# A chain of attention and deformable convolutions: the offset convolutions read an image without padding columns, 512 columns a matmul

## The reference

```python
# layer 2: h = relu(bn1(conv1x1(x, w1))), 64 channels; 27 outputs: 18 offsets and 9 masks
off = conv2d(h, woff, stride 1, padding 1) + boff                # woff: (27, 64, 3, 3)
# layer 3, twice: h = relu(group_norm(x)), 256 channels; 18 offsets
f   = depthwise_conv2d(h, dw, 7x7, 'SAME')
off = conv2d(f, pw, 1x1) + pwb                                   # pw: (18, 256, 1, 1)
# both: every pixel takes 9 bilinear samples of h at its own offsets, then a matrix
y, x = base_y + off[:, :, 0], base_x + off[:, :, 1]
samp = bilinear(h, y, x)                                         # four corners, zero outside the image
out  = einsum('bckhw,ock->bohw', samp, w)
```

## Time and profile before

| | |
|---|---|
| time, median of 3 runs | 6705.33 us (6679.31 to 6709.67) |
| profiled execution: span, first to last instruction | 5987.5 us |
| profiled execution's own time | not given apart from its span; the median is 717.8 us above the span |
| PE busy | 5187.2 us (87%) |
| DVE busy | 4250.2 us (71%) |
| POOL busy | 3228.6 us (54%) |
| ACT busy | 2265.2 us (38%) |
| offset matmuls of layer 3 (L738) | 1792 records, 433.3 us busy |
| offset matmuls of layer 2 (L738) | 192 records, 56.6 us busy |

### The profile page before, as it was taken

One profiled execution on the slowest core, in us unless ns is written; L12 is line 12 of the kernel. 1 busy time (PEld: TensorE's weight loads), 2 busy tenths in 40 slices (PEclk: granted clock), 3 DMA queues, 4 the chain that ended last, 5 costly groups with the idle time before them and its releaser, 6 DMA issues. The chain is left out here.

```text
span 5987.5 us, 83281 instructions
## 1 busy us (share of the span) xinstructions
PE 5187.2 (87%) x24252; PEld 2620.8 (44%) x24252; DVE 4250.2 (71%) x7123; ACT 2265.2 (38%) x4090; POOL 3228.6 (54%) x2826
## 2 busy tenths in 40 slices
PE   7999999997676788878879999999977767888788
PEld 3333333333665544644433333333336655446444
DVE  5888888873223599579858888888732235995798
ACT  2444444441112156235524444444411122662355
POOL 0666666661773277147606666666617732771476
PEclk9999999997787899989989999999977878999899
DMA  1000000001333599579900000000013335995799
GB/s 54 1 1 1 1 1 1 1 1 35 105 105 106 189 410 410 177 272 410 371 32 1 1 1 1 1 1 1 1 37 105 105 110 193 410 410 172 277 410 364
DMA packets 310971, 790.59 MB, mean 132 GB/s; under 512 B 69512, under 2 KB 136401, under 8 KB 310222
## 3 DMA queue, kind: packets, MB, share of 16 engines
q0 software_dynamic: 193536, 679.59, 29.7%
q1 hardware_dynamic: 117198, 107.99, 6.2%
HBM read 701.57 MB, written 85.87 MB: 132 GB/s over the span
## 5 line engine op out<-in xcount | busy, mean ns | idle before, releaser
L615 POOL TENSOR_TENSOR arena<-arena 128x512 f32<-128x512 f32 x960 | 1407.5, 1466 | 828.9 <-ACT arena L1115 764.7
L697 POOL DMA_INDIRECT arena<-corners,arena x1152 | 1086.7, 943 | 993.3 <-POOLq L696 706.7
L1115 ACT ACTIVATE arena<-ps 128x1024 f32<-128x1024 f32 x1024 | 1049.5, 1025 | 1239.2 <-PE ps L840 1209.7
L1564 DVE TENSOR_REDUCE arena<-ps 128x2 f32<-128x1024 f32 x1024 | 1243.3, 1214 | 347.1 <-PE ps L814 347.1
L1046 PE MATMUL ps<-arena 128*128 128x512 f32 x2304 | 1065.3, 606 | 3.3 <-PEq L1043 3.2
L840 PE MATMUL ps<-arena 64*128 64x512 f32 x4096 | 1046.0, 589 | 0.0
L1748 DVE SCALAR_TENSOR_TENSOR ps<-arena,ps 128x256 f32<-128x256 f32 x2304 | 956.9, 483 | 108.1 <-DVEq L1742 69.8
L853 PE MATMUL ps<-arena 128*64 128x512 f32 x4096 | 991.3, 605 | 0.0
L1586 DVE TENSOR_TENSOR arena<-arena 128x512 f32<-128x512 f32 x960 | 890.4, 928 | 62.5 <-ACT arena L1115 62.1
L1269 ACT ACTIVATE ps<-arena 128x256 f32<-128x256 f32 x1152 | 503.1, 469 | 625.4 <-DMA arena<-corners,arena 557.6
L652 POOL DMA_INDIRECT arena<-corners,arena x576 | 546.2, 948 | 338.9 <-issue 173.8
(11 more groups left out here) (132 smaller groups left out, 3708.7 us busy)
## 6 DMA issues: line engine op xcount, KB each, us to landing
corners<-arena SPq DMA_DIRECT2D x256, 256.0 KB, 3.9
arena<-corners,arena POOLq DMA_INDIRECT x1728, 2.8
arena<-in_wd SPq DMA_DIRECT2D x4, 2304.0 KB, 8.3
X<-in_x SPq DMA_DIRECT2D x8, 1024.0 KB, 8.4
corners<-arena SPq DMA_DIRECT2D x128, 64.0 KB, 2.2
out_y<-arena SPq DMA_DIRECT2D x32, 256.0 KB, 5.5
arena<-in_base SPq DMA_DIRECT2D x4, 288.0 KB, 9.2
arena<-in_base SPq DMA_DIRECT2D x2, 432.0 KB, 3.1
```

The lines of the kernel that those rows point to most:

```text
L615: pool.tensor_tensor(SUMS[u % 2][:, 0, :], SUMS[u % 2][:, 0, :], P[n % 4][:, 0, :], ALU.add).then_inc(sum_a, 1)
L697: pool.indirect_dma_start(G3[4 * k + t].rearrange("p a c -> p (a c)"), None, table256, bass.IndirectOffsetOnAxis(ap=IS3[:, k, t:t + 1], ax ...
L1115: af(P[n % 4].rearrange("p h q -> p (h q)"), ps[:, 2 * (n % 2):2 * (n % 2) + 2, :].rearrange("p h q -> p (h q)"), ACT.Exp, scale=float(D) ...
L1564: v.tensor_reduce(mxp[i % 2][:, :, j], ps[:, 4:6, :], AX.X, ALU.max).then_inc(mx_done, 1)
```

## The change

The padding columns go. The image is stored with 64 columns and padded above and below only (`HP2` 66 rows, `HP7` 70 rows), so 8 image rows are 512 contiguous columns whatever `ky` is: `rows` is one matmul of 512 columns per `ky` and half, in one PSUM bank. The missing side columns are handled in the shift: DVE starts with the middle `kx`, which covers all 64 columns, and adds the others only where they stay inside the row (61, 62 or 63 columns in layer 3, 63 in layer 2). ACT writes each chunk once, into the image, and PE's table transposes read the image; the staging tiles and the semaphores `image_ready`, `stage_free` and `h1_free` go. POOL clears only the rows above and below. The loops over chunks on PE and ACT are written out.

```diff
-        HP2 = bot.f32(PW2 * PW2, parts=CB)
-        STG2 = [bot.f32(CHUNK, parts=CB) for _ in range(2)]
+        HP2 = bot.f32(ROWS2 * W, parts=CB)
...
-                    pool.memset(HP7.rearrange("p a n -> p (a n)"), 0.0).then_inc(pool_step, 1)
+                    for at in (0, (H + 3) * W):
+                        pool.memset(HP7[:, :, at:at + 3 * W], 0.0).then_inc(pool_step, 1)
...
-                    pe.wait_ge(image_ready, 1)
-                    pe.sem_inc(image_ready, -1)
-                    for j in range(2):
-                        first = True
-                        for half in range(halves):
-                            for ky in range(ksize):
-                                last = mm(ps[0:ko, 2 + 2 * p + j, 0:n], wts(half, ky),
-                                          img(half)[:, bass.ds((8 * blk + 4 * j + ky) * pw_, n)],
-                                          start=first, stop=(half == halves - 1 and ky == ksize - 1))
-                                first = False
-                        last.then_inc(t_ps, 1)
+                    first = True
+                    for half in range(halves):
+                        for ky in range(ksize):
+                            last = mm(ps[0:ko, 2 + p, :], wts(half, ky), img(half)[:, bass.ds((8 * blk + ky) * W, CHUNK)],
+                                      start=first, stop=(half == halves - 1 and ky == ksize - 1))
+                            first = False
+                    last.then_inc(t_ps, 1)
...
-                with act.Fori(0, NCH // 2 - 1) as n2:
-                    for p in range(2):
-                        norm(2 * n2 + 2 + p, p)
...
-                        for half in range(CH):
-                            padded = HP7[:, half, :].rearrange("p (y x) -> p y x", y=PW7)
-                            af(padded[:, bass.ds(8 * n + 3, 8), 3:3 + W],
-                                   src[:, half, chunk(n)].rearrange("p (y x) -> p y x", x=W), ACT.Relu,
-                                   scale=gsc[:, half:half + 1], bias=gbi[:, half:half + 1]).then_inc(act_step, 1)
...
+                    for n in range(NCH):
                         for half in range(CH):
+                            af(HP7[:, half, (8 * n + 3) * W:(8 * n + 11) * W], src[:, half, chunk(n)], ACT.Relu,
+                               scale=gsc[:, half:half + 1], bias=gbi[:, half:half + 1]).then_inc(stage_ready, 1)
...
-                    for kx in range(ksize):
-                        for j in range(2):
...
-                                dve.wait_ge(chain, 2 * (kx - 1) + j + 1)
...
+                    dve.wait_ge(t_ps, 1)
+                    dve.sem_inc(t_ps, -1)
+                    moved = ps[0:ksize * no, 2 + p, :].rearrange("q (y x) -> q y x", x=W)
+                    rows = tbuf[p].rearrange("q (y x) -> q y x", x=W)
+                    mid = ksize // 2
+                    v.tensor_scalar(rows, moved, sel[:, mid:mid + 1], None, ALU.mult).then_inc(chain, 1)
+                    others = [kx for kx in range(ksize) if kx != mid]
+                    for i, kx in enumerate(others):
+                        dve.wait_ge(chain, i + 1)
+                        to = slice(max(0, mid - kx), W - max(0, kx - mid))
+                        at = slice(max(0, kx - mid), W - max(0, mid - kx))
+                        v.scalar_tensor_tensor(rows[:, :, to], moved[:, :, at], sel[:, kx:kx + 1], rows[:, :, to],
+                                               op0=ALU.mult, op1=ALU.add).then_inc(
+                                                   chain if kx < ksize - 1 else t_ready, 1)
```

More of the change, by code:

```diff
@@ L30 @@
 KK = 9
[L31 removed]
+ROWS2, ROWS7 = H + 2, H + 6
 O2, O3 = 27, 18
@@ L156, in program @@
         hole = dcn.at
-        HP7 = dcn.f32(CH, PW7 * PW7)
+        HP7 = dcn.f32(CH, ROWS7 * W)
         after = dcn.at
@@ L171, in program @@
         stg = Carver(dcn.at)
-        STG3 = [stg.f32(CH, CHUNK) for _ in range(2)]
         TS3 = [stg.f32(4, C) for _ in range(2)]
@@ L625, in _ @@
                 pool.sem_inc(go_pool, -1)
-                pool.memset(HP2, 0.0).then_inc(pool_step, 1)
-                pool.wait_ge(pool_step, 1)
-                pool.sem_inc(pool_step, -1)
+                for at in (0, (H + 1) * W):
+                    pool.memset(HP2[:, at:at + W], 0.0).then_inc(pool_step, 1)
+                pool.wait_ge(pool_step, 2)
+                pool.sem_inc(pool_step, -2)
                 pool.memset(IDX2[:, NT:NT + 5, :], 0).then_inc(pool_step, 1)
@@ L757, in offset_conv @@
                 rows(0, 0)
-                def two(n2):
-                    for p in range(2):
[L760 to L773, removed]
+                for n in range(2, NCH):
+                    table(n, n % 2)
+                    rows(n - 1, (n - 1) % 2)
+                    shifted(n % 2)
                 rows(NCH - 1, 1)
@@ L937, in table2 @@
                     for t in range(4):
-                        last = tr(ps[:, 1, t * CB:(t + 1) * CB], STG2[p][:, t * 128:(t + 1) * 128],
+                        last = tr(ps[:, 1, t * CB:(t + 1) * CB], HP2[:, bass.ds((8 * n + 1) * W + t * 128, 128)],
                                   ident_s[0:CB, 0:CB])
@@ L944, in _ @@
                 conv1(0)
-                offset_conv(table2, lambda half: HP2, 1, PW2, 3, lambda half, ky: woff_s[:, ky, :], T2, O2, sel2_s,
-                            written_out=True)
+                offset_conv(table2, lambda half: HP2, 1, 3, lambda half, ky: woff_s[:, ky, :], T2, O2, sel2_s)
                 pe.drain().then_inc(arrived, 1)
@@ L1161, in _ @@
                 act.sem_inc(go_act, -1)
-                def norm2(n, p):
+                for n in range(NCH):
                     act.wait_ge(h1_ready, 1)
                     act.sem_inc(h1_ready, -1)
[L1166 to L1180, removed]
+                    half = slice(n % 2 * CB, (n % 2 + 1) * CB)
+                    af(HP2[:, (8 * n + 1) * W:(8 * n + 9) * W], ps[half, 0, :], ACT.Relu, scale=bnf1[half, 0:1],
+                       bias=bnf1[half, 1:2]).then_inc(stage_ready, 1)
                 act.drain().then_inc(arrived, 1)
@@ L1227, in _ @@
                     act.sem_inc(go_act, -1)
-                    def norm3(n, p):
-                        act.wait_ge(stage_free, 1)
-                        act.sem_inc(stage_free, -1)
+                    for n in range(NCH):
                         for half in range(CH):
-                            af(STG3[p][:, half, :], src[:, half, chunk(n)], ACT.Relu,
-                                   scale=gsc[:, half:half + 1], bias=gbi[:, half:half + 1]).then_inc(stage_ready, 1)
-                        for half in range(CH):
-                            padded = HP7[:, half, :].rearrange("p (y x) -> p y x", y=PW7)
-                            af(padded[:, bass.ds(8 * n + 3, 8), 3:3 + W],
-                                   src[:, half, chunk(n)].rearrange("p (y x) -> p y x", x=W), ACT.Relu,
-                                   scale=gsc[:, half:half + 1], bias=gbi[:, half:half + 1]).then_inc(act_step, 1)
[L1240 to L1246, removed]
+                            af(HP7[:, half, (8 * n + 3) * W:(8 * n + 11) * W], src[:, half, chunk(n)], ACT.Relu,
+                               scale=gsc[:, half:half + 1], bias=gbi[:, half:half + 1]).then_inc(stage_ready, 1)
                     act.drain().then_inc(arrived, 1)
@@ L1433, in group_norm, with table_and_offsets @@
                 dve.sem_inc(dve_step, -1)
-            def table_and_offsets(stage, pv, off, base, ksize, pw_, tbuf, sel, no):
+            def table_and_offsets(stage, pv, off, base, ksize, tbuf, sel, no):
                 def tiles(p):
```

47 lines of the change are left out of this document (10 added, 37 removed).

## The result

The change takes 6653.53 us (median of 8 runs, 6634.97 to 6662.17) against 6685.63 us (8 runs, 6677.64 to 6709.67): a ratio of 0.9943, 95% interval 0.9928 to 0.9958, 32.1 us less. The forecast was 36.4 us less: 6669 us, in a range of 6642 to 6700, from a median of three runs before of 6705.33. Over eight runs that median is 19.7 us lower; counted from there the forecast is 6649.2 us, and the time lies 4.3 us above it.

What follows compares the result with a forecast made beforehand. PE was taken to bound the layer-3 offset stages and SP's table DMAs the layer-2 ones. Terms of -37.4 (PE), +1.6 (DVE) and -0.6 (layer 2) gave -36.4 us: from 6705.3 to 6669 us, range 6642 to 6700.

Steps and rivals of the forecast that it cites:

- Fewer columns, layer 3: PE's layer-3 `rows`, 28 records of 512 columns for 56 of 280: 1.17 us less a chunk, -37.4 us in all.
- Rival D: Layer-3 `rows`: a 512-column record costs 472 ns, so PE gains nothing and the time is 6706 us; chance 0.05.
- the transfers: Layer-3 table tiles: 8.2 us to move and 6.9 to issue, both under a step of 13.8 us, so 0.
- The shift on DVE: Last `block` of each layer-3 stage, now seven chained instructions: +0.4 us a stage, +1.6 us in all.
- the price of a chained wait: DVE's layer-3 `block`: each chained instruction waits 0.15 us, a figure taken from the chain in `corners`.
- Rival C: DVE's `block`: chained waits are free, so the tails give 3.6 us in place of costing 1.6: 6664 us; chance 0.10.
- ACT and POOL: ACT's dropped second pass and POOL's shorter clears were hidden already, so they gain 0.
- the pace: Layer-2 stage: SP's 64 DMAs, 54.76 us without a break, set its length; -0.3 us a stage, -0.6 us in all.
- rival A: Layer-2 stage: less PE work lowers the clock; at 0.50 throughout 22.7 us more a stage, 6714 us; chance 0.08.
- the prediction's own sign: Layer-2 stage expected at 67 to 68 us; more than 3 us off would show the forecast wrong.
- that waits stay while work goes: Layer-2 stage: the change removes PE work and leaves the waits, so the low clock level may come earlier.
- Around the span: Outside the profiled span of 5987.5 us: 717.8 us to the median, not in the trace, taken as unchanged.

Runs made afterwards that it cites:

- Experiment 2: Kernel before with only the four layer-3 offset stages in the new form, layer 2 as before: 5952.15 us, ratio 0.9925 to the kernel before.
- experiment 8: The change with every layer-3 `rows` done twice into the same bank: 6346.74 us, 391.2 more than the change on the same chip.
- experiment 7: The change with ACT's second activations (into unread tiles) and POOL's full clears put back: 5959.32 us, ratio 0.9935 to the kernel before.
- experiment 9: The change with layer-2 `rows` weights zero-padded to 128 rows and 128 columns, image on 128 partitions: 6618.76 us, ratio 0.9903 to the kernel before.
- 10: The change with layer-2 `rows` weights padded to 128 x 128 and table writes split between SP and ACT: 6620.33 us, ratio 0.9909 to the kernel before.
- experiment 6: The change with layer-2 table writes issued half from SP, half from ACT: 5958.41 us, ratio 0.9936 to the kernel before.
- after: Profile of the change itself against the kernel before: this execution took 6634.97 us, median of 8 runs 6653.53 us, ratio 0.9943.
- experiment 3: Kernel before with only the two layer-2 offset stages in the new form, layer 3 as before: 5993.91 us, ratio 0.9993 to the kernel before.
- experiment 4: The change with DVE adding each shift in two halves of four rows, 14 instructions each waiting two back: 5958.11 us, ratio 0.9938 to the kernel before.
- experiment 5: The change again, unedited, on a chip of the short kind: 5955.55 us, ratio 0.9933 to the kernel before.
- 12: The change with layer-2 `rows` weights zero-padded to 128 columns only, 64 rows kept: 6642.40 us, ratio 0.9931 to the kernel before.

## Why the prediction was right, and where not

- **Fewer columns, layer 3: right.** Term -1.17 us a chunk; measured 13.21 - 12.01 = 1.20, -38.4 in all. Experiment 2 has the whole gain there, and experiment 8 shows that nothing else holds the step. Rival D is gone, and so is any doubt about the transfers, which the prediction put at 0: in the steady steps PE never waits for a tile.
- **The shift on DVE: wrong sign, small.** The term +0.4 us for the last block measured -0.2 (5.57 to 5.37). The step that failed is the price of a chained wait, taken from `corners` as 0.15 us where it is 0.04. Rival C had the direction and not the size. Both terms together are -39.2, and the stages fell by 39.5.
- **ACT and POOL: right**, 0 (experiment 7).
- **Layer 2: the pace was right in part, the clock failed.** The prediction let SP's 64 DMAs set the pace and took the clock as unchanged. SP's DMAs are the floor: with the clock up they take 55 of 65 us (experiment 9), and only then does a second queue help (10). At 0.57 halving them on SP changed nothing (6): there PE's work at the granted clock sets the stage. In the profiles the old form takes 69.95, 71.03, 69.95, 71.33, 72.77 and 70.59 us, mean 70.9; the change's form (after, 3, 4, 5, 7, 8) 67.94 to 78.22 us, mean 74.9 of 12. That is +3.9 a stage, +7.9 in all, in place of -0.6.
- **Layer 2: rival A, smaller.** Of the 3.9 us, 1.5 are longer issue on SP (seven of the twelve have 56.4 to 58.9 us, the old form 54.0 to 54.8) and 2.5 come behind its last DMA (10.5 us on average, against 8.0). This is rival A at a clock of 0.54 to 0.73 (the old form has 0.64 to 0.72) and not at 0.50 throughout, so it takes back a fifth of the gain and does not outweigh it. By the prediction's own sign, a layer-2 stage off by more than 3 us, this part was wrong. The size stays open: the old form was profiled on chips of the short kind alone, where the change's ten stages average 75.7 us; the runs of experiment 3 do not confirm a loss (-9.6 to +1.2 us by their interval), while experiment 2, with layer 2 left old, lies 6.0 us below experiment 4 on the same chip, in ranges that overlap. Why the new form sits lower stays open too: that waits stay while work goes was the prediction's argument, and no run tests it by itself.
- **The sum.** -39.5 + 7.9 = -31.6 us by the stages, measured -32.1 and -35.5. Against the forecast of -36.4, PE gave 1.0 us more and DVE 2.4, and layer 2 took 8.5: three misses, two of them against the third. That stages and medians agree to a few microseconds is partly luck, since the eight runs of the change alone span 27 us.
- **Around the span: wrong.** "I take it as unchanged" did no harm, but 1.8 us lie there, not 717.8. The forecast of a difference survived because the 700 us belong to stages that the change doesn't touch, and so carry over just the same. A change to the sampling stages, costed from that profile, would have been sized for the wrong kind of chip.

## What to carry to other kernels

When a profiled span and the medians differ by more than a few microseconds, find out which stages differ before building on either: the two may come from different chips. A stage in which PE is busy at a clock of 0.5 to 0.7 may be bound by that clock, even where a queue issues beside it with hardly a break; the test is to take the queue's work away and see what PE does, and to do it again once the clock is up, for here the queue was the next limit. Where its matmuls use half the rows and columns, padding the weights with zeros to the full array streams no more columns and can be worth more than removing work: here it took a stage to 65.3 us, from 70.9 on a chip of the same kind and 74.9 over all profiles.

## What the runs showed of the hardware

- The same program takes 5991 and 5998 us on two chips and 6686 and 6690 us on two others, the difference all in the sampling stages (414 and 585 us in layer 2). On the long kind PE stands still between its matmuls there for 40.0 of 300 us with nothing in the profile to wait for.
- Busy is not enough for the upper clock: 38 us without a gap at 0.50 (experiment 6). With the records of `rows` on 128 x 128 weights the stage's clock is 0.79 to 0.84 (experiment 9), with 64 x 128 it is 0.62 to 0.64 (12), with the change's 64 x 81 it is 0.54 to 0.73.
- A chained DVE instruction on a PSUM source of 488 to 504 elements starts 0.77 us after the last at a duration of 0.73 (experiment 5), where the chain in `corners` has 0.15 us between the earlier trace rows.
